# Products without a reader in TensorE's waits, a third pass without a next group, and a table worked out in two parts

## What is computed

```
h = tok(x, itok)                    # word row + position + type, LayerNorm; gated with a word vector
h = h + L0_attn(ln(h))              # linear attention: 12 heads of 16, cumulative sums over the tokens
h = h + L0_ffn(ln(h))               # a router keeps part of the tokens for attention, mean of the rest; FFN 192 -> 768 -> 192, gelu
h = h + L1_attn(ln(h))              # softmax attention, 12 heads, low-rank q, k, v
h = h + L1_ffn(ln(h))               # gate -> 2 of 8 experts, each 192 -> 768 -> 192, gelu
return h

# tok
e = word_emb[sents] + pos_emb + type_emb[0]
b = (e - mean(e)) * rsqrt(var(e) + eps) * gamma + beta
a = sigmoid(b @ gate_w + gate_b)
g = wvec[wids] @ g2b_w.T + g2b_b
return (1 - a) * b + a * g
```

## Time and profile before

| | |
|---|---|
| three runs | 877.9, 879.14, 880.11 us |
| median | 879.14 us |
| the profiled execution | 878.32 us, its span 876.3 us |
| PE busy | 729.2 us, 83% of the span |
| DVE busy | 520.1 us, 59% |
| ACT, POOL busy | 303.9 us, 243.4 us |
| mean granted TensorE clock | 0.923 of full |
| the chain that ended last | PE 59%, DVE 21%, issue 5%, ACT 5%, DMA 4%, POOL 4% |

### The profile page before, as it was taken

How to read it: one execution, slowest core, us unless ns; L and a number is a source line. 1 busy time by engine, 2 the same in 40 slices (tenths; PEclk the granted TensorE clock), 3 DMA queues, 4 the chain that set the end, 5 groups by cost and what they waited for, 6 DMA issues and landing times.

```text
span 876.3 us, 15714 instructions
## 1 busy us (share of the span) xinstructions
PE 729.2 (83%) x5548; PEld 561.7 (64%) x5549; DVE 520.1 (59%) x1766; ACT 303.9 (35%) x700; POOL 243.4 (28%) x302
## 2 busy tenths in 40 slices
PE   1888777989678998867899976868878989999993
PEld 0546465566457565656666555757756989998892
DVE  7558757873678785668877476891434553333330
ACT  0033232624333263433244344223323433333330
POOL 5332200460013246001443300142000453333332
PEclk9999989999978999998899997797956999999998
DMA  7960000000000000000122000019301233222220
GB/s 251 411 247 1 1 1 1 19 8 1 1 1 28 27 19 8 1 2 1 37 35 9 1 3 1 1 55 344 90 1 29 43 73 47 38 37 38 36 35 8
DMA packets 29894, 43.63 MB, mean 50 GB/s; under 512 B 5355, under 2 KB 24597, under 8 KB 29830
## 3 DMA queue, kind: packets, MB, share of 16 engines
q1 hardware_dynamic: 19250, 30.87, 10.2%
q0 software_dynamic: 8752, 9.07, 6.5%
q10 hardware_dynamic: 1828, 2.84, 0.9%
HBM read 21.36 MB, written 22.09 MB: 50 GB/s over the span
## 4 chain that ended last, share of the span: by engine, by line
PE 59%; DVE 21%; issue 5%; ACT 5%; DMA 4%; POOL 4%; ACTq 1%; SPq 1%; POOLq 0%; DVEq 0%
PE qa L1898 26%; PE qc L1898 24%; PE qa L1901 4%; PE qc L1901 4%; DMA out<-qk_T 3%; DVE mx L1487 2%; POOL arena_w L438 1%; DVE st L1058 1%; ACT big L814 1%; DVE ctxT L1442 1%; DMA mu_row<-in_mu 1%; DVE qk_T L1493 1%; DVE arena_b L1425 1%; ACTq L641 1%; DVE arena_e L1299 1%
## 5 line engine op out<-in xcount | busy, mean ns | idle before, releaser
L1898 PE MATMUL qc<-arena_w,big 128*128 x468 | 82.8, 327 | 1.4 <-DVE qk_T L1877 1.4
L1898 PEld LDWEIGHTS qc<-arena_w,big 128*128 128x128 f32 x468 | 75.1, 190 | 2.1 <-issue 2.0
L1898 PE MATMUL qa<-arena_b 128*128 128x128 f32 (+2 forms) x688 | 73.1, 287 | 2.9 <-DVE att L1503 2.1
L1898 PEld LDWEIGHTS qa<-arena_b 128*128 128x128 f32 (+2 forms) x688 | 64.5, 191 | 11.5 <-DVE att L1503 2.5
L1898 PE MATMUL qa<-arena_e,nT 128*128 128x192 f32 (+2 forms) x256 | 69.9, 429 | 1.1 <-DVE ga L1369 0.7
L1024 ACT ACTIVATE big<-qa,arena_b 128x128 f32<-128x128 f32 x156 | 43.1, 375 | 74.9 <-PE qc L1898 68.4
L611 POOL DMA_INDIRECT out<-qk_T x39 | 61.0, 1565 | 20.6 <-issue 11.1
L1866 DVE COPY arena_b<-qc 128x256 f32<-128x256 f32 x39 | 16.6, 426 | 81.3 <-PE qc L1901 81.3
L1898 PEld LDWEIGHTS qa<-arena_e,nT 128*128 128x128 f32 x256 | 47.2, 200 | 22.9 <-issue 12.9
L474 POOL TENSOR_TENSOR rs_a<-rs_a,minus_half 128x8 f32<-128x8 f32 x4 | 6.6, 1644 | 175.5 <-DVE rs_a L1336 175.5
L1898 PE MATMUL qc<-qk_T 32*128 32x128 f32 (+1 forms) x680 | 33.5, 321 | 17.9 <-DVE qk_T L1493 13.5
(11 more groups left out here) (390 smaller groups left out, 1598.5 us busy)
## 6 DMA issues: line engine op xcount, KB each, us to landing
slots<-xk SPq DMA_DIRECT2D x1, 13192.0 KB, 41.8
arena_e<-in_w SPq DMA_DIRECT2D x8, 579.0 KB, 8.1
arena_w<-in_w SPq DMA_DIRECT2D x8, 576.0 KB, 9.4
qk_T<-slots SPq DMA_DIRECT2D x39, 97.0 KB, 1.9
out<-hb SPq DMA_DIRECT2D x16, 96.0 KB, 1.7
arena_e<-in_w_l SPq DMA_DIRECT2D x1, 804.0 KB
arena_e<-in_W ACTq DMA_DIRECT2D x1, 768.0 KB
out<-qk_T POOLq DMA_INDIRECT x39, 3.5
```

The costliest lines, as they stand in the source:

```text
L1898: return nc.tensor.matmul(o, l, r, start=start, stop=stop)
```

## The change

The change has three parts. First, all calls that prepare group `ta + 1` now stand under `if ta + 1 < NG`, on every engine, so that the third pass has none of them; the indices lose their padding, SP and POOL wait for 4 groups' gathers instead of 5, and PE's waits on `g_diff` go in that pass. Second, PE gets `hold(bank, n)`: n products of 256 columns into 32 partitions of a bank of qa or qc. They wait for no one, and no one reads them. There are 24 in each pass and 31 in `back`, 103 in all, each lot right before a call. Third, `table` is cut in two, `table` and `table_rows`, and in `back` the second call goes ahead of `rows_out`, its first part after the fourth tile's evacuation and its second part after the fifth's.

```
+            def hold(bank, n):
+                for _ in range(n):
+                    mm(bank[0:32, 0:256], ident[:, 0:32], w_1q[:, 0, 0:8, :].rearrange("p h d -> p (h d)"))
@@ PE, joint @@
                 o_T(tb, 1)
+                hold(QC[:, 3, :], 1)
                 logits(tb, 2)
                 av(ta, 3)
+                hold(QA[:, 2, :], 2)
                 max_T(tb, 2)
                 ob_T(ta, 3)
                 logits_T(tb, 2)
+                hold(QA[:, 2, :], 3)
                 av1(tb, 2)
+                hold(QC[:, 3, :], 1)
                 o_T(tb, 2)
...
                 max_T(tb, 3)
+                hold(QC[:, 3, :], 5)
                 logits_T(tb, 3)
+                hold(QA[:, 2, :], 1)
                 n3_T(ta, 0)
                 n3_T(ta, 1)
                 av1(tb, 3)
+                hold(QC[:, 3, :], 1)
                 o_T(tb, 3)
...
                 select(ta)
+                hold(QC[:, 3, :], 2)
                 queries(ta)
+                hold(QC[:, 3, :], 1)
                 counts(tb)
                 select_T(ta)
                 route_logits(ta, 0)
-                words_T(ta + 1)
+                if ta + 1 < NG:
+                    words_T(ta + 1)
                 route_logits(ta, 1)
                 gates_T(tb)
-                word_vectors(ta + 1)
+                if ta + 1 < NG:
+                    word_vectors(ta + 1)
+                hold(QC[:, 3, :], 5)
                 mix(ta, 0)
...
+                hold(QC[:, 3, :], 2)
                 selected(ta, 0)
@@ PE, back @@
+                hold(QC[:, 3, :], 7)
                 n4_T(tb, 0)
+                hold(QC[:, 3, :], 2)
                 up_half(tb, 0, 0)
...
                 logits(tb, 0, True)
+                hold(QA[:, 3, :], 4)
                 max_T(tb, 0, True)
+                hold(QA[:, 3, :], 1)
                 logits_T(tb, 0, True)
                 logits(tb, 1, True)
                 av1(tb, 0, True)
+                hold(QC[:, 3, :], 2)
                 max_T(tb, 1, True)
+                hold(QC[:, 3, :], 1)
                 logits_T(tb, 1, True)
                 o_T(tb, 0, True)
+                hold(QC[:, 3, :], 1)
                 logits(tb, 2, True)
...
                 o_T(tb, 2, True)
+                hold(QC[:, 3, :], 2)
                 av1(tb, 3, True)
                 w(tb, "h_l1", 3 * 2 + 2)
                 x_T(0, 0, 1)
                 o_T(tb, 3, True)
                 x_T(1, 1, 1)
+                hold(QC[:, 1, :], 4)
                 w(tb, "h_l1", 3 * 3 + 2)
                 pe.wait_ge(route, R_EARLY)
                 up(0, 0)
@@ DVE, joint @@
                 mask(ta, 2, 0)
-                token_dot(ta + 1)
+                if ta + 1 < NG:
+                    token_dot(ta + 1)
                 mask(ta, 2, 1)
...
                 mixed(ta, 1)
-                token_diff(ta + 1)
+                if ta + 1 < NG:
+                    token_diff(ta + 1)
                 route_norm(ta, 0)
                 route_norm(ta, 1)
-                token_mix(ta + 1)
+                if ta + 1 < NG:
+                    token_mix(ta + 1)
                 mix_in(ta, 0)
-                ln1_stats(ta + 1)
+                if ta + 1 < NG:
+                    ln1_stats(ta + 1)
                 mix_in(ta, 1)
                 contexts(ta, 0)
                 contexts(ta, 1)
-                ln1_apply(ta + 1)
+                if ta + 1 < NG:
+                    ln1_apply(ta + 1)
                 rows_out(tb, 0)
@@ DVE, back @@
                 evacuate(4, 4, 0)
+                table(EARLY, MT, NG)
                 evacuate(5, 5, 0)
+                table_rows(EARLY, MT)
+                evacuate(6, 0, 1)
                 rows_out(tb, 0)
                 rows_out(tb, 1)
-                table(EARLY, MT, NG)
-                for tile in range(RING, EARLY):
+                for tile in range(RING + 1, EARLY):
                     evacuate(tile, tile % RING, tile // RING)
```

88 lines of the change are left out of this document (59 added, 29 removed).

## The result

| | before | changed |
|---|---|---|
| median | 879.62 us (877.9 to 880.21, 4 runs) | 850.75 us (848.72 to 852.94, 4 runs) |
| ratio | | 0.9675, 95% interval 0.9647 to 0.9703 |
| profiled execution, span | 876.3 us | 848.8 us |
| mean granted clock | 0.923 | 0.972 |
| time at 0.50 within the span | 134.9 us | 46.9 us |

A forecast was written before the change was run, and what follows sets the result against it. PE's low clock, in pieces of thin products and waits, DVE's late preparation and PE in the tiles were taken to bound it; 3.3 + 1.1 + 9.8 + 3.5 + 9.5 + 2.3 = 29.5 us off gave 850 us, range 843 to 864.

The forecast's parts named there:

- first pass: From av1 to logits_T, 2.5 us from lifting the low clock, and 0.8 for later pieces up to mix: 3.3 us.
- second pass: Already at full clock from av1 to logits_T; 1.1 us for the later pieces.
- third pass: Clock 1.8, 2.4 and 0.6 us up to mix; dropped preparation 1.0 for token_dot, 4.0 for late calls: 9.8 us.
- start of back: Piece of 10.2 us at 0.50: PE's chain from the first up_half and transposes ahead run at full clock, 3.5 us.
- attention: back's attention, 37.6 us at 0.50, goes to full clock: 2.8, 3.2, 1.7 and 1.8 us, 9.5 in all.
- tail: In back, PE's 2.34 us wait for the seventh tile's rows goes when the second table is split: 2.3 us.
- The cost of the holds: 103 held products, 0.45 us each at full clock, 46 us of PE, fit in PE's waits and cost nothing.
- The clock: Pieces at 0.50 with holds inside go to full clock; those without, about kq and the gate, may stay or shift.
- lies beside other work: nothing: Third pass: the rest of the dropped preparation (gathers, token_stats, POOL's roots, PE's words_T) gains nothing.
- (a): Rival: clock lifted only in part, back's attention keeps its 9.5 us and holds overrun by about 1: 860 us; chance 0.14.
- (b): Rival: holds fit but change nothing, only preparation, 5.0, and tail, 2.3, are left: 871 us; chance 0.07.
- (c): Rival: clock stays low and holds, 0.9 us each, overrun the waits, so the kernel is slower: 891 us; chance 0.04.

The follow-up runs named there:

- e11: The changed kernel with every lot of held products twice as long, 206 in all, on a third chip: 892.69 us.
- e1: The kernel before with the 103 held products alone, at all 25 places, and no other edit: 856.62 us, ratio 0.978.
- e9: The changed kernel with POOL waiting for DVE's last application of ln5 before scale_k of sequence 1 in all three passes, on a third chip: 869.35 us, ratio 0.9805.
- e5: The changed kernel again with no edit, on another chip: 848.1 us, ratio 0.9659.
- e4: The kernel before with only the 31 held products of back and none in the passes: 867.6 us, ratio 0.9904.
- e3: The kernel before with only the second table cut in two and moved ahead of the rows: 877.44 us, ratio 1.0004.
- e2: The kernel before with only the third pass's preparation left out: 875.0 us, ratio 0.9985.
- e8: The changed kernel with POOL in the third pass waiting for DVE's last application of ln5 before scale_k of sequence 1: 847.11 us, ratio 0.9655.

## Why the prediction was right

The terms, against the stage table:

| term | forecast | changed against before |
|---|---|---|
| up to the first pass | 0 | 1.0 |
| first pass | 3.3 | 3.7 |
| second pass | 1.1 | 1.6 |
| third pass | 9.8 | 8.2 |
| start of back | 3.5 | 3.4 |
| attention | 9.5 | 8.7 |
| tail | 2.3 | 1.0 |
| sum | 29.5 | 27.5 |

**The cost of the holds, nothing.** Shown at one place, `max_T` 2.88 us after `logits` with four of them; four more there are 1.8 us by the forecast's price and delay it by 1.57 (e11), so the cover was what the rows said. For all 103 it is not shown. By the means of its chip e1 has 83 us less at 0.50 than before and is 18.6 us faster, 0.22 for each, where the scatter of before has 0.26; the 3 us between may be what holds cost elsewhere. At the low clock they cost nearly twice as much: in e9's first pass the two before `selected` take 1.92 us, at 0.50, which take 1.05 at full in e5.

**The clock.** Shown by e1 and e4: the holds alone bring 43 us at 0.50 in the trace, where the runs of before have 107 to 151, and 17.8 us by the medians of that chip. The clock's terms of the sum, 3.3 + 1.1 + 4.8 + 3.5 + 9.5 = 22.2, fit the 88 us less at 0.50 at 0.26 each, 23 us.

One of the forecast's own signs of being wrong did come: a window with holds is still at 0.50, the one around `select`, 552.70 to 556.10, in which held products run. No term had put much there, so it cost little.

**The terms were read from one execution.** Attention, 9.5, is right against that one. But the same calls took 34.1 and 35.1 us there in e3 and e2, not 40.7, and against these the term would be 2 to 3. The first two passes are off the other way: with holds they take 142.1 and 142.3 to 142.4 us in e1 and e5 to e8, which is 5.6 and 3.3 us under before, where 3.3 and 1.1 were forecast; in the changed kernel's own trace each had one piece at 0.50 more. The third pass of before, 139.2, takes 137.0 in e3 and e4 with the same calls. The sum held because the profiled execution was ordinary in its total at 0.50, though not in where it lay, and because these errors offset each other. That wasn't known when it was made; to that extent it was luck.

**The third pass.** `token_dot` gave 1.1 (forecast 1.0), the stretch to `logits_T` 1.8 (1.8), to `select` 2.4 (2.4), to `mix` 3.5 and behind it 1.0 (0.6 and 4.0 together). The preparation "lies beside other work: nothing" was the step that failed: taking POOL's root away cost 1.6 us of the lead in this trace, and giving the wait back made the pass 2.3 us shorter in e8, the clock's share included. POOL's row behind the root would have told it, had I asked what moves up when the root goes.

**The tail.** PE's wait went, and PE was 2.5 us further ahead at the ninth tile (the earlier trace rows calls its products the seventh tile's, after the number of the evacuation). 1.4 us of that lead was lost again by the end, 0.6 by the eleventh tile, 0.4 at the fifteenth and the rest over the loop. What waits there wasn't tested. That the old wait also brought a low piece in some executions wasn't foreseen.

Of the rivals, (a), lifted in part, is nearest to what is left: the short pieces at `select`, with holds in them. (b) and (c) are out by e1.

## What to carry to other kernels

Cut the trace at the edges of the granted clock and hold the same stage of several executions side by side before a term is taken from one; where the clock moves, the mean over a span says more than where a piece lies. Products without a reader paid here where the wait was longer than they were, and beyond it cost most of their length (1.57 of 1.8 us before `max_T`, 6.1 of 9.9 over the attention). What they bring is to be measured on more than one chip. When an instruction is taken out of an engine's stream, look at what that engine now does earlier, and beside whom: here one wait on POOL gave back up to 2.3 us.

## What the hardware did that was not expected

- TensorE's granted clock: the same calls of `back`'s attention had 38, 12 and 12 us at 0.50 in three traces (before, e3, and e2, whose third pass is shorter), and 28 runs of before differed by 12 us, in step with their time at 0.50 (correlation 0.94).
- Four DVE instructions of 128x192 took 1.25 us alone, 2.21 us with POOL's root and then its wide product beside them, and 2.94 us with it beside them from the start; POOL's own took 2.3 us each time.
- On one chip the signals of PE's transposes after `mix` came 1.2 to 3.9 us after their recorded ends, in each pass of four kernels, and in the ten other traces, from other chips, within 0.02 us. The change gained 16 us there instead of some 30. The cause stays open: no trace of before was taken on that chip.
